# Expert numbers kept in registers, halves at the first load and the last chunk, one more engine that stores: a mixture-of-experts kernel on one core

## The chip, the core and the metric

The kernel runs on one core of a Trainium2 chip. Five engines run their own instruction streams and meet only at semaphores: TensorE (PE: matmuls and transposes; PEld is its loading of weights), VectorE (DVE), ScalarE (ACT), GpSimd (POOL) and SyncE (SP), which here issues most of the DMAs. The metric is the time of one execution in microseconds (us) on the device; lower is better. The median of three runs of the kernel before is 500.7 us (499.16 to 501.32).

## What is computed

For 4096 tokens of 256 features in 64 groups of 64 (`x`), a layer whose weight depends on the group, then a mixture of 8 experts of which each token takes 2, then a shared MLP, and the residual:

```python
# cond: h = x @ W_base.T + b_base + 2 * sum_e cond[b, e] * (x @ As[e].T) @ Bs[e].T
# As: (8, 16, 256)   Bs: (8, 256, 16)   cond_8: (64, 8)
scores = softmax(h @ gate_w.T)                      # 8 experts
topk_w, topk_i = top_k(scores, 2)
topk_w = topk_w / (topk_w.sum(-1) + 1e-20) * 2.5
g = silu(h @ w_gate[e]) * (h @ w_up[e])             # F = 352
y = sum over the 2 experts: topk_w * (g @ w_down[e])
out = x + y + (silu(h @ sw_gate) * (h @ sw_up)) @ sw_down   # 704 wide
```

## The kernel before

Every product is built from three passes over operands split in a high and a low part: `three_pass` at lines 281 to 283 (high by high, high by low, low by high). The high part is a cast by ScalarE, the low part a subtraction by VectorE. TensorE's stream has four stages.

1. Start (to about 11 us). WARM = 14 transposes of `ident` run while the first DMAs are under way (L617). Then come the transposes of `a_raw` (L622), of the first 512 tokens of x (`turn_x(0)`, L586, all of feature half k = 0 and then of k = 1), of the small inputs, the product of the base weight with the gate (L640), and the first projection. ScalarE casts each transposed half (`x_high`, L856) and then copies `gate_t`, which L640 needs. `b_raw` is turned at L650. SyncE issues x, `base_raw`, `g_raw`, `b_row`, `bias`, the second 512 tokens of x and the shared weights in this order; ScalarE's queue issues `a_raw`, `cond_in` and the two halves of `b_raw`. These two halves are read in runs of 16 floats (64 bytes).
2. The projection of the eight groups of 512 tokens (NG = 8), then the shared MLP of the first five groups (30 units: six chunks of 128 columns, the last one 64 wide, for each group), with the routing worked out beside it.
3. The expert blocks (about 182 to 412 us). The routed rows lie in NBLK = 71 blocks of 128 rows, each of one expert, whose number is in `blk_e`. One step (`e_step`) is: turn the product `g` of the block before (`e_turn_g`, L772, 3 transposes), gate and up of this block (`e_gate_up`, 12 matmuls at L281 to L283), and the down product of the block before (`e_down`, L800 and L802, 6 matmuls), which waits for `gt_l` of VectorE's L1335. Behind the gate matmuls a step also loads the next block's expert number into a register (`expert_of`), except in the last step of a turn and in the last block. Blocks 0 and 1 are written out; then a loop (`pe.Fori`) runs 5 turns of TURN = 12 steps (blocks 2 to 61), and at the head of each turn two expert numbers are loaded. Blocks 62 to 70 are written out behind two such loads.
4. The shared MLP of the last three groups (18 units), with VectorE adding up the routed rows (`sums`, L1369) beside it. The last unit is chunk 5 of group 7: `silu` (L954), the product (`mul`, L1260), the high part (`g_high`, L962), the low part (`g_low`, L1269), 8 matmuls (`down`, L722 and L723), the additions into `acc` (`final`, L1285 and twice L1281), and three stores by SyncE (L457). A chunk of 64 rows has its high part in rows 0 to 63 and its low part in rows 64 to 127 of `gt_h`, so it needs only two matmuls per 128 tokens.

The order on each engine is written out by hand; nothing is planned by a compiler.

Of the kernel before, what the change touches and what calls it, by code (L numbers as in the profile page):

```python
# [5 lines left out]
F32 = mybir.dt.float32  # L6
# [5 lines left out]
ALU = mybir.AluOpType  # L12
# [3 lines left out]
P = 128  # L16
# [5 lines left out]
def adaln_moe(nc, x, cond, w_base, b_base, lora_a, lora_b, gate_w, w_gate, w_up, w_down,  # L22
# [7 lines left out]
    K = D // P  # L30
# [9 lines left out]
    TG = GT // P  # L40
    NG = T // GT
# [13 lines left out]
    WARM = 14  # L55
# [22 lines left out]
    with ExitStack() as ctx:  # L78
# [135 lines left out]
        s_xin = [sem(f"s_xin{i}") for i in range(2)]  # L214
        s_tx, s_txh, s_txl = sem("s_tx"), sem("s_txh"), sem("s_txl")
# [28 lines left out]
        G_B, U_B, Y_B = [bank[0], bank[2]], [bank[1], bank[3]], bank[4:6]  # L244
        RANK_B, PERM_B = bank[6], bank[7]
# [57 lines left out]
        def _(sp):  # L303
# [51 lines left out]
            sp.dma_start(b_row[:], b_base.rearrange("(k p) -> k p", p=P)).then_inc(s_dc, 16)  # L355
            sp.dma_start(bias[:, 0:D], b_base.rearrange("(a o) -> a o", a=1).broadcast_to([P, D])).then_inc(s_dbias, 16)
            load_x(1)
# [221 lines left out]
        def _(pe):  # L579
# [44 lines left out]
            turn_x(0)  # L624
# [119 lines left out]

            order = [(j, c) for j in range(NG) for c in range(NC)]
# [65 lines left out]

            before = expert_of(0)
            expert = e_gate_up(0, 0, before, 1)
            down(*order[NPRE - 1])
            e_step(1, 1, before, expert, None)
            n_turns = (NBLK - 3) // TURN
            with pe.Fori(0, n_turns) as q:
                before = expert_of(q * TURN + 1)
                expert = expert_of(q * TURN + 2)
                for s in range(TURN):  # L820
                    before, expert = expert, e_step(
                        q * TURN + (2 + s), s % 2, before, expert, q * TURN + (3 + s) if s + 1 < TURN else None)
            i = n_turns * TURN + 2
            before, expert = expert_of(i - 1), expert_of(i)
# [12 lines left out]
            for last in order[-2:]:  # L837
                down(*last)

        @block.scalar  # L840
        def _(sc):
            sc.dma_start(a_raw[:], lora_a.rearrange("e r c -> (e r) c")).then_inc(s_da, 16)
            sc.dma_start(cond_in[:], cond).then_inc(s_dcond, 16)
            for k in range(K):
                sc.dma_start(b_raw[:, k, :].rearrange("p (e r) -> p e r", e=E),
                             lora_b[:, k * P:(k + 1) * P, :].rearrange("e o r -> o e r")).then_inc(s_db, 16)
# [116 lines left out]

            def r_word_high(i):
# [60 lines left out]
            for u in range(UP, UP + (NG - NPG) * NC):  # L1025
# [3 lines left out]
                if c in (1, 2) and j + 1 < NG:  # L1029
                    split(j + 1, c - 1)  # L1030

        @block.vector
        def _(v):
# [256 lines left out]

            def r_word_low(i):
# [93 lines left out]
            for n in range((NG - NPG) * NC):  # L1385
# [36 lines left out]
```

## Time and profile before

| | us |
|---|---|
| median of three runs | 500.7 |
| the profiled execution | 496.86 |
| its span, first to last instruction | 494.7 |
| TensorE matmul busy | 487.9 (99%) |
| VectorE busy | 349.6 (71%) |
| ScalarE busy | 262.2 (53%) |
| GpSimd busy | 220.3 (45%) |

The granted clock is full over the whole span. Busy time of TensorE is that of pipelined matmuls, whose ends are modelled, so it does not mean that the engine is at its peak; it does mean that gaps are few. The profiled execution took 3.8 us less than the median of the three runs.

### The profile page before, as it was taken

How to read it: one execution, taken by the hardware profiler on the slowest of the kernel's cores; microseconds unless marked ns; L12 is line 12 of the kernel's file. 1: busy time of each engine (PE TensorE's matmuls, PEld its weight loads, DVE VectorE, ACT ScalarE, POOL GpSimd, SP SyncE). 2: the span in 40 equal slices, each digit the busy share in tenths (PEclk: the TensorE clock that was granted, in tenths of full speed). 3: DMA queues.
4: the chain of work that ended last, by engine and by line, in shares of the span. 5: the costliest groups of instructions: out<-in, count | busy, mean ns of one | idle time of the engine just before them, and what ended most of it. 6: DMA issues, size and time to landing. Idle time of an engine off the chain costs nothing.

```text
span 494.7 us, 9766 instructions
## 1 busy us (share of the span) xinstructions
PE 487.9 (99%) x3071; PEld 449.3 (91%) x3072; DVE 349.6 (71%) x783; ACT 262.2 (53%) x525; POOL 220.3 (45%) x231
## 2 busy tenths in 40 slices
PE   8999999999999999999999999999999999999996
PEld 7999988888888899999999999999999999888886
DVE  3557866888887556766876776676676666379895
ACT  3577876666563445565555554555555543535322
POOL 2052238655541453565776556555555652211100
PEclk9999999999999999999999999999999999999999
DMA  8398569472222244543444444444444451699932
GB/s 230 112 294 243 172 185 316 150 219 85 44 85 44 86 98 126 121 127 107 127 119 116 116 127 117 108 127 118 111 121 123 117 112 56 176 383 302 384 139 85
DMA packets 104936, 74.53 MB, mean 151 GB/s; under 512 B 61946, under 2 KB 99844, under 8 KB 104900
## 3 DMA queue, kind: packets, MB, share of 16 engines
q1 hardware_dynamic: 95780, 55.21, 38.5%
q0 software_dynamic: 6816, 18.62, 12.8%
q10 hardware_dynamic: 2304, 0.26, 0.5%
q8 instruction: 17, 0.28, 0.3%
q14 instruction: 19, 0.16, 0.1%
HBM read 40.25 MB, written 20.32 MB: 122 GB/s over the span
## 4 chain that ended last, share of the span: by engine, by line
PE 94%; DVE 3%; issue 1%; DMA 1%; ACT 1%; DVEq 0%
PE bank L281 23%; PE bank L282 22%; PE bank L283 22%; PE bank L800 10%; PE bank L802 5%; PE bank L772 5%; PE bank L586 2%; DVE acc L1369 1%; DMA xin<-in_x_dram 1%; PE bank L598 1%; PE bank L594 1%; PE bank L595 1%; ACT gt_h L962 1%; PE bank L722 1%; DVE bank L1258 1%
## 5 line engine op out<-in xcount | busy, mean ns | idle before, releaser
L561 POOL DMA_INDIRECT y_rows<-y_sb,dst_i x71 | 69.9, 985 | 82.8 <-DVE y_sb L1344 82.8
L281 PE MATMUL bank<-w_all,rt_h 128*128 x284 | 97.5, 343 | 0.0
L283 PE MATMUL bank<-w_all,rt_l 128*128 x284 | 91.6, 323 | 0.0
L282 PE MATMUL bank<-w_all,rt_h 128*128 x284 | 91.5, 322 | 0.0
L555 POOL DMA_INDIRECT rows<-x_halves,tok_i x71 | 68.6, 967 | 25.3 <-issue 21.1
L800 PE MATMUL bank<-w_all,gt_h 128*128 (+1 forms) x213 | 78.1, 397 | 0.1
L962 ACT CAST gt_h<-bank 128x512 fp32r<-128x512 f32 (+1 forms) x48 | 28.1, 585 | 86.5 <-DVE bank L1258 77.1
L281 PE MATMUL bank<-xs_h,sg_h 128*128 128x512 f32 x176 | 70.4, 400 | 0.0
L282 PE MATMUL bank<-xs_l,sg_h 128*128 128x512 f32 x176 | 68.9, 391 | 0.0
L283 PE MATMUL bank<-xs_h,sg_l 128*128 128x512 f32 x176 | 68.7, 390 | 0.0
L1331 DVE TENSOR_TENSOR g<-bank,act 128x352 f32<-128x352 f32 x71 | 37.2, 524 | 40.2 <-ACT act L983 38.8
L978 ACT CAST gt_h<-bank 128x384 fp32r<-128x384 f32 x71 | 34.0, 479 | 59.5 <-PE bank L772 59.4
L1344 DVE TENSOR_REDUCE y_sb<-bank 128x256 f32<-128x512 f32 x71 | 49.0, 691 | 17.3 <-PE bank L802 16.2
L802 PE MATMUL bank<-w_all,gt_l 128*128 (+1 forms) x213 | 59.6, 280 | 0.0
L501 POOL TENSOR_TENSOR w_all<-w_own,w_all 128x704 fp32r<-128x704 f32 (+2 forms) x32 | 42.8, 1360 | 32.6 <-ACT w_all L874 32.6
L969 ACT COPY rt_w<-turned 128x256 uint16<-128x256 uint16 x71 | 34.6, 488 | 40.7 <-PE bank L283 29.2
L282 PEld LDWEIGHTS bank<-w_all,rt_h 128*128 128x128 f32 x284 | 53.6, 189 | 0.0
L281 PEld LDWEIGHTS bank<-w_all,rt_h 128*128 128x128 f32 x284 | 53.5, 188 | 0.1
L283 PEld LDWEIGHTS bank<-w_all,rt_l 128*128 128x128 f32 x284 | 53.4, 188 | 0.0
L1335 DVE TENSOR_TENSOR gt_l<-bank,gt_h 128x384 fp32r<-128x384 f32 x71 | 39.5, 557 | 11.5 <-ACT gt_h L978 4.6
L507 POOL TENSOR_TENSOR xs_l<-xs_w,xs_h 128x512 fp32r<-128x512 f32 x14 | 18.3, 1310 | 65.5 <-ACT xs_h L896 65.5
L800 PEld LDWEIGHTS bank<-w_all,gt_h 128*128 128x128 f32 (+1 forms) x213 | 40.0, 188 | 6.9 <-issue 0.6
(183 smaller groups left out, 1114.4 us busy)
## 6 DMA issues: line engine op xcount, KB each, us to landing
pick<-y_rows SPq DMA_DIRECT2D x16, 512.0 KB, 7.8
xin<-in_x_dram SPq DMA_DIRECT2D x8, 512.0 KB, 4.9
x_halves<-x_half SPq DMA_DIRECT2D x8, 512.0 KB, 3.3
w_own<-in_L_ffn_w_gate_dram SPq DMA_DIRECT2D x8, 352.0 KB, 4.3
w_own<-in_L_ffn_w_up_dram SPq DMA_DIRECT2D x8, 352.0 KB, 4.7
y_sb<-in_x_dram SPq DMA_DIRECT2D x5, 512.0 KB, 3.5
base_rows<-y_sb SPq DMA_DIRECT2D x5, 512.0 KB, 2.8
acc<-base_rows SPq DMA_DIRECT2D x5, 512.0 KB, 7.3
```

Of the source, the lines that this page charges most:

```text
L281: pe.matmul(o, lh, rh, start=start, stop=False, skip_group_check=skip)
L282: pe.matmul(o, lh, rl, start=False, stop=False, skip_group_check=skip)
L283: return pe.matmul(o, ll, rh, start=False, stop=stop, skip_group_check=skip)
L501: pool.tensor_tensor(lo, own_ap, hi.bitcast(F32), ALU.subtract).then_inc(s_wlo, 1)
L555: pool.indirect_dma_start(rows[i % 3][:], None, x1_dram, bass.IndirectOffsetOnAxis(ap=tok_i[:, i:i + 1], axis=0)).then_inc(s_row[i % 3], 16)
L561: pool.indirect_dma_start(y_dram, bass.IndirectOffsetOnAxis(ap=dst_i[:, i:i + 1], axis=0), y_sb[:, i % 4, :], None).then_inc(s_sc[i % 4], 16)
L800: pe.matmul(YE[par][:, 0:2 * D].rearrange("p (h d) -> p h d", h=2), gt_h[par][0:n, cols], both, start=(c == 0), stop=False, skip_group_che ...
L802: mm = pe.matmul(YE[par][:, 0:D], gt_l[par][0:n, cols], high, start=False, stop=(c == FC - 1), skip_group_check=True)
L969: sc.copy(words[:, :, :, 1], turned[i % 2][:, K:2 * K, :]).then_inc(s_rhi, 1)
L1331: v.tensor_tensor(g[:, 0:F], EU[:, 0:F], act[:, 0:F], ALU.mult).then_inc(s_g, 1)
L1335: v.tensor_tensor(gt_l[i % 2][:, 0:FC * P], TB[:, 0:FC * P], gt_h[i % 2][:, 0:FC * P].bitcast(F32), ALU.subtract).then_inc(s_gl, 1)
L1344: v.tensor_reduce(y_sb[:, i % 4, :], YE[i % 2][:, 0:2 * D].rearrange("p (h d) -> p d h", h=2), AX.X, ALU.add).then_inc(s_y, 1)
```

## The change

- TensorE keeps two expert numbers in two registers of its own. The last step of a turn now loads the next block's number too, as block 1 does, and the two numbers are moved to the kept registers at the end of a turn and read from them at the head of the next; the two loads at the head of each turn, and those behind the loop, are gone.
- x's first 512 tokens come in two DMAs of 256 tokens with a semaphore each, and are turned token tile by token tile (k inside), so that the first four transposes need the first DMA only. WARM goes from 14 to 12.
- SyncE's queue: x (two halves), `base_raw`, the second 512 tokens, `b_raw` (two), `bias`. ScalarE's: `a_raw`, `cond_in`, `g_raw`, `b_row`.
- Product, high part and low part of the last chunk are each made in two halves of 256 columns, the halves in two PSUM banks (3 and 2); the eight matmuls wait for the halves in turn.
- Of the last three stores the middle one (tile 2) is issued by ScalarE.

```diff
-    WARM = 14
+    WARM = 12
+        LAST_B = [U_B[(NC - 1) % 2], G_B[(NC - 1) % 2]]
-            load_x(0)
+            for h, got in enumerate((s_xfirst, s_xin[0])):
+                sp.dma_start(xin[0][:, h * HT:(h + 1) * HT, :],
+                             x_rows[h * HT * P:(h + 1) * HT * P, :].rearrange("(t p) d -> p t d", p=P)).then_inc(got, 16)
             sp.dma_start(base_raw[:], ...).then_inc(s_dw, 16)
-            sp.dma_start(g_raw[:], gate_w).then_inc(s_dg, 16)
-            sp.dma_start(b_row[:], ...).then_inc(s_dc, 16)
+            load_x(1)
+            for k in range(K):
+                sp.dma_start(b_raw[:, k, :]..., lora_b[:, k * P:(k + 1) * P, :]...).then_inc(s_db, 16)
             sp.dma_start(bias[:, 0:D], ...).then_inc(s_dbias, 16)
-            load_x(1)
...
-            for n, (first, end) in enumerate(((0, 2), (2, 3), (3, 4))):
+            for n, (first, end) in ((0, (0, 2)), (2, (3, 4))):
...
-            turn_x(0)
+            pe.wait_ge(s_xfirst, 16)
+            for t in range(TG):
+                if t == HT:
+                    pe.wait_ge(s_xin[0], 16)
+                for k in range(K):
+                    mm = pe.transpose(TX[k][:, t * P:(t + 1) * P], xin[0][:, t, k * P:(k + 1) * P], ident[:])
+                    if t == TG - 1:
+                        mm.then_inc(s_tx, 1)
...
+            def down_last():
+                j, c = NG - 1, NC - 1
+                u, p = unit(j, c), c % 2
+                for h in range(2):
+                    pe.wait_ge(s_gl, u + 1 + h)
+                    for t in range(2 * h, 2 * h + 2):
+                        ...
+                    mm.then_inc((s_first, s_D)[h], 1)
...
+            def keep(*es):
+                for r, e in zip(kept, es):
+                    pe.reg_mov(r, pe.to_reg(e))
+            def as_kept():
+                return [pe.snap(r, min_val=0, max_val=E - 1) for r in kept]
-            e_step(1, 1, before, expert, None)
+            keep(expert, e_step(1, 1, before, expert, 2))
             with pe.Fori(0, n_turns) as q:
-                before = expert_of(q * TURN + 1)
-                expert = expert_of(q * TURN + 2)
+                before, expert = as_kept()
                 for s in range(TURN):
-                    ... q * TURN + (3 + s) if s + 1 < TURN else None)
+                    ... q * TURN + (3 + s))
+                keep(before, expert)
-            before, expert = expert_of(i - 1), expert_of(i)
+            before, expert = as_kept()
...
+            def g_high_last(h):
+                sc.wait_ge(s_g, u + 1 + h)
+                sc.wait_ge(s_D, u - 1)
+                sc.copy(gt_h[p][0:HALF, cols], LAST_B[h][0:HALF, cols]).then_inc(s_gh, 1)
+            sc.wait_ge(s_fin, 2 * (NG - 1) + 2)
+            sc.dma_start(out_rows[r:r + P, :]..., acc[NG - 1][:, 2:3, :]).then_inc(s_out, 16)
...
+            def mul_last(h):
+                v.wait_ge(s_act, u + 1)
+                v.tensor_tensor(LAST_B[h][0:HALF, cols], G_B[p][HALF:P, cols], act[HALF:P, cols], ALU.mult).then_inc(s_g, 1)
+            def g_low_last(h):
+                v.wait_ge(s_gh, u + 1 + h)
+                v.tensor_tensor(gt_h[p][HALF:P, cols], LAST_B[h][0:HALF, cols], gt_h[p][0:HALF, cols].bitcast(F32),
+                                ALU.subtract).then_inc(s_gl, 1)
```

## Rows read from the trace of the kernel before

**Rows 1.** The page, chain of work that ended last, by engine.

```profile
PE 94%; DVE 3%; issue 1%; DMA 1%; ACT 1%; DVEq 0%
```

**Rows 2.** TensorE's waits: who waited for whom, us in total, times, longest.

```profile
PE bank L772 <- issue: 1.2, 4, 0.5
```

**Rows 3.** Timeline of the start: start, us, engine, line, operation, [idle before <-releaser].

```profile
1.47 3.25 PE L617 MATMUL bank<-ident 128*128 128x128 f32 x14 [1.47 <-POOL ident L472]
1.85 1.23 ACTq L845 DMA_DIRECT2D b_raw<-in_L_cond_Bs_dram  x2
5.34 1.87 PE L586 MATMUL bank<-ident,xin 128*128 128x128 f32 x8 [0.19 <-DMA xin<-in_x_dram]
7.25 0.58 ACT L856 CAST xt_h<-bank 128x512 fp32r<-128x512 f32 x1 [0.17 <-PE bank L586]
...
8.11 0.96 PE L640 MATMUL bank<-gate_t,base_raw 128*128 128x8 f32 x8
...
11.84 0.38 PE L650 MATMUL bank<-ident,b_raw 128*128 128x128 f32 x2
```

**Rows 4.** DMA views: b's two halves (KB, us to landing); SyncE's queue from 0 to 4.

```profile
b_raw<-in_L_cond_Bs_dram ACTq DMA_DIRECT2D x1, 64.0 KB, 4.8
...
b_raw<-in_L_cond_Bs_dram ACTq DMA_DIRECT2D x1, 64.0 KB, 8.4
...
q1 hardware_dynamic: 299, 0.31, 22.0%
```

**Rows 5.** Windows of two steps, TensorE: stretch and its length, busy (x), clock, DMA, GB/s.

```profile
184.91:192.34 7.43, 6.90 (x44) 1.00 0.57 160
...
225.43:232.55 7.12, 6.82 (x44) 1.00 0.49 128
265.58:272.48 6.90, 6.83 (x45) 1.00 0.49 131
305.51:312.54 7.03, 6.86 (x44) 1.00 0.43 116
345.64:352.64 7.00, 6.84 (x44) 1.00 0.48 122
385.75:392.37 6.62, 6.62 (x44) 1.00 0.43 117
```

**Rows 6.** Timeline, the low part and the next transposes, at three places.

```profile
226.30 0.56 DVE L1335 TENSOR_TENSOR gt_l<-bank,gt_h 128x384 fp32r<-128x384 f32 x1
...
229.02 0.54 PE L772 MATMUL bank<-ident,g 128*128 128x128 f32 x3 [0.30 <-issue]
...
386.62 0.56 DVE L1335 TENSOR_TENSOR gt_l<-bank,gt_h 128x384 fp32r<-128x384 f32 x1
...
388.88 0.49 PE L772 MATMUL bank<-ident,g 128*128 128x128 f32 x3
...
407.22 0.56 DVE L1335 TENSOR_TENSOR gt_l<-bank,gt_h 128x384 fp32r<-128x384 f32 x1
...
409.08 0.49 PE L772 MATMUL bank<-ident,g 128*128 128x128 f32 x3
```

**Rows 7.** Queues of instruction fetches: the whole span (page), then 230 to 388 us.

```profile
q8 instruction: 17, 0.28, 0.3%
...
q14 instruction: 8, 0.07, 0.1%
```

**Rows 8.** Timeline of the end.

```profile
489.26 0.68 DVE L1269 TENSOR_TENSOR gt_h<-bank,gt_h 64x512 fp32r<-64x512 f32 x1 [0.65 <-ACT gt_h L962]
...
489.99 0.39 PE L722 MATMUL bank<-sd_h,gt_h 128*128 128x256 f32 x1 [0.31 <-DVE gt_h L1269]
...
491.45 0.75 DVE L1281 TENSOR_TENSOR acc<-bank,acc 128x256 f32<-128x256 f32 x2
491.56 1.39 SPq L457 DMA_DIRECT2D out_dram<-acc  x3
```

**Rows 9.** Windows at the end: busy of five engines (x), clock, DMA share, GB/s.

```profile
493.00:493.50 0.50, 0.00 (x0) 0.00 (x0) 0.00 (x0) 0.00 (x0) 0.00 (x0) 1.00 1.11 385
```

More of the change, by code:

```diff
@@ L40, in adaln_moe @@
     TG = GT // P
+    HC = GT // 2
+    HT = TG // 2
     NG = T // GT
@@ L810, in e_step @@
                 return e_next
+            kept = [pe.alloc_register(f"expert{n}") for n in range(2)]
+            def keep(*es):
[3 more added lines that the diff above has]
+                return [pe.snap(r, min_val=0, max_val=E - 1) for r in kept]
             before = expert_of(0)
@@ L814, in _ @@
             down(*order[NPRE - 1])
-            e_step(1, 1, before, expert, None)
+            keep(expert, e_step(1, 1, before, expert, 2))
             n_turns = (NBLK - 3) // TURN
             with pe.Fori(0, n_turns) as q:
-                before = expert_of(q * TURN + 1)
-                expert = expert_of(q * TURN + 2)
+                before, expert = as_kept()
                 for s in range(TURN):
-                    before, expert = expert, e_step(
-                        q * TURN + (2 + s), s % 2, before, expert, q * TURN + (3 + s) if s + 1 < TURN else None)
+                    before, expert = expert, e_step(q * TURN + (2 + s), s % 2, before, expert, q * TURN + (3 + s))
+                keep(before, expert)
             i = n_turns * TURN + 2
-            before, expert = expert_of(i - 1), expert_of(i)
+            before, expert = as_kept()
             for n in range(i, NBLK):
@@ L836, in _ @@
                 up(j, c)
-            for last in order[-2:]:
-                down(*last)
+            down(*order[-2])
+            down_last()
         @block.scalar
@@ L843, in _ @@
             sc.dma_start(cond_in[:], cond).then_inc(s_dcond, 16)
-            for k in range(K):
-                sc.dma_start(b_raw[:, k, :].rearrange("p (e r) -> p e r", e=E),
-                             lora_b[:, k * P:(k + 1) * P, :].rearrange("e o r -> o e r")).then_inc(s_db, 16)
+            sc.dma_start(g_raw[:], gate_w).then_inc(s_dg, 16)
+            sc.dma_start(b_row[:], b_base.rearrange("(k p) -> k p", p=P)).then_inc(s_dc, 16)
             sc.wait_ge(s_ident, 1)
@@ L1024, in _ @@
             e_high(NBLK - 1)
-            for u in range(UP, UP + (NG - NPG) * NC):
+            for u in range(UP, UP + (NG - NPG) * NC - 1):
                 j, c = NPG + (u - UP) // NC, (u - UP) % NC
@@ L1030, in _ @@
                     split(j + 1, c - 1)
+            silu(NG - 1, NC - 1)
+            for h in range(2):
+                g_high_last(h)
+            sc.wait_ge(s_fin, 2 * (NG - 1) + 2)
+            r = (NG - 1) * GT + 2 * P
+            sc.dma_start(out_rows[r:r + P, :].rearrange("(t p) d -> p t d", p=P), acc[NG - 1][:, 2:3, :]).then_inc(s_out, 16)
         @block.vector
@@ L1384, in _ @@
                        (7, 2): [(7, 5, 8), (4, 0, 3)], (7, 3): [(4, 4, 8)]}
-            for n in range((NG - NPG) * NC):
+            for n in range((NG - NPG) * NC - 1):
                 j, c = NPG + n // NC, n % NC
@@ L1396, in _ @@
                     sums(*some_of)
+            for h in range(2):
+                mul_last(h)
+            for h in range(2):
+                g_low_last(h)
             v.wait_ge(s_mix, TOPK * TG * (NG - NPG))
```

11 lines of the change are left out of this document (10 added, 1 removed).

## The prediction

> **What bounds the kernel now.** I read the page's chain of work that ended last first: 94% of it is TensorE [rows 1]. So what the change can give is what TensorE's stream loses somewhere, plus the ends, where TensorE has not yet begun or is already done. TensorE's list of waits names few losses in the middle: 1.2 us of "issue" in 4 places before L772, that is, waits for nothing that another engine or a DMA does [rows 2]. The timelines of both ends and windows of equal work around the loop's turns give the sizes.
>
> **The loop's turns.** A window over two steps (from one step's transposes to those of the step after next) shows what a turn's head costs. Behind the loop, where two expert numbers are loaded as well but nothing jumps back, two steps take 6.62 us. The four jumps back take 7.12, 6.90, 7.03 and 7.00, together 28.05 against 26.48: 1.57 us over. The entry to the loop takes 7.43, 0.81 over [rows 5]. Together 2.38 us. Half of it is the gap, half the slower start behind it: three transposes take 0.54 behind a gap and 0.49 (of which the next matmuls cover more) elsewhere [rows 6].
>
> Is it the loads? From the end of the low part, on which `e_down` waits, to the next transposes it is 229.02 - 226.86 = 2.16 us at a turn; 388.88 - 387.18 = 1.70 behind the loop, with two loads and no gap; and 409.08 - 407.78 = 1.30 in a step whose `e_down` came late, with neither loads nor jump [rows 6]. I read this so: the instruction stream goes on from the wait in `e_down`, and needs at most 1.30 us for six matmuls and the way to the transposes; two loads, the loop's compare and jump, and the arithmetic on the loop's register add 0.86 or more. TensorE itself arrives after 1.70, so about 0.46 must go for the gap to vanish. The change takes away two loads with their address arithmetic and adds four register moves. Bounds: if the loads carry nothing, the gain is 0 (or below: a few moves more, 0.1 each at most for four jumps and the entry, -0.5); if they carry 0.46 or more, all 2.38 goes. The row behind the loop says that loop control alone is at least 2.16 - 1.70 = 0.46, so the loads' share lies between 0 and 2.16 - 0.46 less the matmuls' own issue. Twelve to fifteen instructions in that 1.30 can hardly fill it, since TensorE takes 0.12 for each there anyway; I take 0.3 per load and its arithmetic, 0.6 for two, and 0.1 back for the moves: the stream is then ready at 1.66, just ahead of TensorE. I enter 2.2 of 2.38. The twelfth step's new load lies behind the gate matmuls as those of the other eleven, which show no loss.
>
> A rule of the Trainium skill speaks against this. "Runtime: NRT & Kernel Launch", section Instruction fetch mechanics, says that code is prefetched in sequence and that a taken jump to code outside the window stalls until the page is fetched; the stall would then be the jump's and stay. In this trace the only queue of instruction fetches from 230 to 388 us is q14 with 8 packets, while q8, with 17 packets of 16 KB over the span, has none there; so no fetch by TensorE goes with the jumps, if q8 is its queue [rows 7]. "Advanced Engine Details and Errata", section Control Flow Timing, has about 108 ns for compare-and-branch, and the Runtime page about 200 ns for one register load (from HBM, not SBUF); an estimate by these two is 0.4 less per turn and 2.16 - 0.4 + moves = 1.8, still a small gap and the slower start, and the loop would give about 0.9.
>
> **The start.** TensorE turns x from 5.34, when the whole DMA has landed, in 8 slots of 0.23 (1.87), and ScalarE's second cast ends at 7.83; behind it come `gate_t` and L640 at 8.11, and from there TensorE runs without a gap [rows 3]. After: twelve transposes instead of fourteen (3.25 for 14) and `a_raw`'s two end near 4.55. The first 256 tokens are 256 packets of 1 KB, and SyncE's queue had moved 299 by 4.0 us [rows 4]; the whole of x (512) landed near 5.3. I put the first half's landing at 4.5, between 4.0 and 5.3. Four slots run to 5.5, the second half is there, four more end near 6.6. Feature half k = 0 is now whole only one slot before k = 1, so ScalarE's two casts run one behind the other, 6.4 to 7.45, against 7.83: 0.38 us gained, not the 0.6 by which the transposes end earlier. If the first half lands with the second, the eight slots stay where they are and k = 0 comes later: the second cast ends near 8.1, 0.27 lost. If the faster pace seen from L640 on (0.96 for 8) comes later than before because less ran ahead of it, up to 0.2 goes as well.
>
> `b_raw` moves from ScalarE's queue (issues from 1.85) behind 1.28 MB on SyncE's, issued from about 2.7. Its landing took 4.8 and 8.4 us [rows 4], the second while it shared the DMA engines with SyncE's bulk. It is needed at 11.84 - 0.38 = 11.46 [rows 3]. With 8.4 from 3.3 it lands at 11.7, 0.25 late; with 4.8 at 8.1. In the new order it stands alone between the second x and `bias`, so I take nothing, and keep -0.25. `g_raw` and `b_row` stand behind 130 KB on ScalarE's queue and are needed near 6.6; `base_raw` is issued 0.45 later and needed near 7: nothing. SyncE's shared weights are needed only after 20 us. Whatever is gained here is carried on, since TensorE bounds all that follows.
>
> **The end.** TensorE has a gap of 0.31 before L722, waiting for L1269, and its first slot is 0.23 instead of 0.12; with the slot that ran out before it the last eight matmuls could begin at 489.42 + 0.12 = 489.53 instead of 489.99, and the loss is 0.46 + 0.11 = 0.57 [rows 8]. Halves: VectorE 0.33 to 0.42 for 256 columns (two L1281 in 0.75) instead of 0.68 for 512 (L1269) [rows 8]; for ScalarE I take 0.42 too. Three whole steps of 512 columns end at 489.94, so they began near 487.9. From there the product's first half ends at 488.32, the high part's near 488.8, the low part's near 489.25 and the second low part's near 489.6, needed at 490.0. So TensorE has no gap: 0.57 gained. The stores: SyncE issues three in 1.39, 0.46 each, from 491.56; the third goes at 492.49, though its rows were ready at 492.2 [rows 8]. With ScalarE issuing the middle one, the third issue goes at 491.63 + 0.03: 0.83 earlier. But the 512 KB take 1.36 us at 385 GB/s [rows 9] from the first store on, and that one moves by 0.57 only. I take 0.57 for the end, 0.83 as its upper bound. (The Trainium skill, "DMA: Bandwidth & Descriptors", section Issuing engines are not separate DMA queues, says that a second issuing engine saves issue time only; that row agrees so far.) If the halves cost a bank wait or a slow semaphore, 0.3 is left.
>
> **Sum.** 2.2 + 0.38 + 0.57 = 3.15 us off the profiled 496.86, that is 493.7. The profiled execution lies 3.84 under the median of 500.7, and I take the same difference off the median: 497.5 (-0.6%). A measurement of this kernel can tell about 0.5%, 2.5 us, from no change, so the forecast is just beyond it.
>
> **Rivals.**
> 1. The jump and not the loads makes the gaps (or the moves cost what the loads did). For it: the two loads behind the loop cost nothing seen. Against it: the entry, which jumps back from nowhere, loses most. Then the loop gives 0.5 and the sum is 1.45: 499.3. Chance 0.23.
> 2. The first half lands with the second: the start loses 0.27 instead, sum 2.5: 498.2. For it: both halves run over the same 16 engines, and all of x took until 5.3 though 299 of 512 packets were through at 4.0. Against: those 299 already include a whole half. Chance 0.15.
> 3. Slower: `b_raw` on SyncE's queue. TensorE's stream stops at L650 until it lands, and with it `lora_out` and all that follows. At 11.46 it begins to cost; from 14.6, 11.3 us after its issue, it eats all 3.15 us. The 8.4 seen says no, but a queue that stands still for 2048 packets of 64 B would also hold the shared weights behind it. With the landing at 16: 502.1. Chance 0.04.
> 4. The change does nothing that can be seen, because the gains in TensorE's stream are given back by a wait for rows or weights from DRAM that don't come earlier. TensorE's list of waits shows no such wait now [rows 2]. 500.5, chance 0.06.
> The forecast keeps 0.52. Its own range, from the bounds above and the spread of the runs, is 496.3 to 498.8; with the rivals I give 495.8 to 500.2. Faster by over 0.5% (under 498.2): most of the forecast, half of rival 2 and a little of rival 1, 0.54. Within 0.5%: 0.42. Slower: 0.04.
>
> **What would show it.** Windows over two steps across each jump should read 6.62 to 6.7 and the entry no more than 6.7; if they stay at 7.0, rival 1. The transposes of x should begin before 4.8 and L640 near 7.75; a wait for x's first half until 5.3 is rival 2. L650 should follow its neighbour without a gap; else rival 3. The last chunk's L722 should have no gap, the third store's issue should begin near 491.66 less what came earlier, and the data should end 0.57 earlier relative to TensorE's last unit. The prediction is wrong if the two-step windows away from the jumps grow, since they are 99% of the time.

## The result and the profile after

The changed kernel takes 493.74 us (median of 6 runs, 492.86 to 499.03); the kernel before, beside it on the same chip, 499.93 (497.01 to 501.32). The ratio is 0.9895, 95% interval 0.9855 to 0.9935. The forecast was 497.5, and 493.74 lies 2.1 us under the low end of its range. Ratios and differences of means, here and below, leave out executions more than 1.5% above the fastest of the same kernel; medians are of all. The six spans of the changed kernel are 495.0, 491.5, 491.0, 492.3, 497.2 and 491.4: four close together and two that are 3.5 and 6 us longer. The profiled execution is one of the two long ones (496.81, span 495.0), so its span of 495.0 beside the 494.7 of before says nothing until it is taken apart.

The start, from the timeline (start, us, engine, line, operation, [idle before <-releaser]); it answers to [rows 3]:

```profile
4.57 3.03 SPq L366 DMA_DIRECT2D bias<-in_L_cond_b_base_dram  x1
...
4.70 1.65 PE L640 MATMUL bank<-ident,xin 128*128 128x128 f32 x8
...
6.27 1.07 ACT L895 CAST xt_h<-bank 128x512 fp32r<-128x512 f32 x2 [0.96 <-PE bank L640]
...
11.33 0.38 PE L668 MATMUL bank<-ident,b_raw 128*128 128x128 f32 x2
```

x is turned from 4.70 instead of 5.34, both casts run one behind the other until 7.34 (forecast 7.45), and the transposes of `b_raw` stand at 11.33 without a gap, 0.51 earlier than in [rows 3]. TensorE's first expert step begins at 184.25; it was 184.74.

The loop, from windows of TensorE alone (stretch and length, busy (x), granted clock, DMA share, GB/s); they answer to [rows 5]. Each is two steps, except those of 5.07 and 5.08, which are one:

```profile
184.25:191.12 6.87, 6.87 (x44) 1.00 0.55 155
191.12:197.91 6.79, 6.79 (x45) 1.00 0.34 97
197.91:202.98 5.07, 3.47 (x23) 1.00 0.63 137
...
222.85:229.47 6.62, 6.62 (x44) 1.00 0.44 119
262.57:269.19 6.62, 6.62 (x44) 1.00 0.45 120
299.03:304.11 5.08, 3.46 (x23) 1.00 0.49 142
304.11:310.76 6.65, 6.65 (x43) 1.00 0.28 86
343.79:350.40 6.61, 6.61 (x45) 1.00 0.43 119
```

The turns' heads read 6.62, 6.62, 6.65 and 6.61 where they read 7.12, 6.90, 7.03 and 7.00 (these windows begin one step earlier than those of [rows 5]; the step behind each head is 3.30 too): the heads cost nothing now. The entry reads 6.87 instead of 7.43. But the next two steps take 6.79, and then one step alone takes 5.07 instead of 3.30; a second such step comes at 299. TensorE's list of waits has both:

```profile
PE bank L803 <- DVE g L1394: 3.2, 2, 1.6
```

The last two batches below turn on these long steps. Here is the one at 198 (timeline of ScalarE, VectorE and TensorE):

```profile
198.16 0.41 PE L286 MATMUL bank<-w_all,rt_h 128*128 x1
...
200.76 0.46 ACT L1028 ACTIVATE act<-bank 128x352 f32<-128x352 f32 x1 [1.44 <-PE bank L288]
...
202.40 0.53 DVE L1394 TENSOR_TENSOR g<-bank,act 128x352 f32<-128x352 f32 x1 [2.46 <-issue]
...
202.98 0.55 PE L803 MATMUL bank<-ident,g 128*128 128x128 f32 x3 [1.60 <-DVE g L1394]
```

In step 2 the first gate matmul begins at 187.89 and `act` at 189.14, 1.25 later; here `act` begins 2.60 later. So what is late is the signal of TensorE's own gate product, 1.35 us, and then the up product's; VectorE and TensorE's next transposes only pass it on. TensorE's matmul records of this step stand 0.16 apart as always, and their ends are modelled: the records don't show where in the step TensorE stood.

The end, from the timeline; it answers to [rows 8]:

```profile
489.58 0.76 DVE L1351 TENSOR_TENSOR gt_h<-bank,gt_h 64x256 fp32r<-64x256 f32 x2
...
490.21 0.28 PE L288 MATMUL bank<-sd_h,gt_l 128*128 128x256 f32 x1
490.33 0.28 PE L772 MATMUL bank<-sd_h,gt_h 128*128 128x256 f32 x1
...
491.69 0.74 DVE L1333 TENSOR_TENSOR acc<-bank,acc 128x256 f32<-128x256 f32 x2
491.80 1.01 SPq L467 DMA_DIRECT2D out_dram<-acc  x2
492.14 0.38 ACTq L1082 DMA_DIRECT2D out_dram<-acc  x1
```

The last eight matmuls follow the unit before without a gap. From its last matmul to the span's end it is 4.79 (495.0 - 490.21), where it was 494.7 - 489.41 = 5.29: 0.50 gained.

Taken apart: 0.51 (start), 1.55 (four heads, 28.05 - 26.50), 0.38 at the entry and the steps behind it (0.70 less in step 1, from 4.09 to 3.39, and 0.32 more in steps 2 to 4, from 9.95 to 10.27), 0.50 (end), and 0.34 for one step at 405 us that took 3.64 before and 3.30 now: 3.28, so 494.7 - 3.28 = 491.4. That is the span of the four short executions (491.0 to 492.3), which I read as those without a long step; only the long one was profiled. It has two, 3.55 us: 495.0.

### The profile page after: what moved, and what is told of

Same layout as the page of the kernel before. It is cut to its first block, busy times and chain, and to the rows that moved or that the text cites. A ratio compares the mean times of both kernels' runs of the same rounds, so it can differ in the third digit from the quotient of the medians.

```text
span 495.0 us, 9758 instructions
## 1 busy us (share of the span) xinstructions
PE 486.6 (98%) x3069; PEld 448.7 (91%) x3070; DVE 349.8 (71%) x785; ACT 261.8 (53%) x526; POOL 220.3 (45%) x231
## 4 chain that ended last, share of the span: by engine, by line
PE 93%; DMA 2%; DVE 2%; issue 1%; ACT 1%; SPq 0%; POOL 0%; DVEq 0%; another core or an unknown queue 0%; POOLq 0%
PE bank L286 22%; PE bank L288 22%; PE bank L287 22%; PE bank L831 10%; PE bank L833 5%; PE bank L803 5%; DMA pick<-y_rows 1%; PE bank L596 1%; PE bank L608 1%; PE bank L604 1%; DMA y_rows<-y_sb,dst_i 1%; PE bank L605 1%; PE bank L741 1%; PE bank L740 1%; DVE acc L1432 1%
## 5 line engine op out<-in xcount | busy, mean ns | idle before, releaser
L1407 DVE TENSOR_REDUCE y_sb<-bank 128x256 f32<-128x512 f32 x71 | 49.0, 690 | 17.4 <-issue 9.7
```

The source lines that it names most:

```text
L1407: v.tensor_reduce(y_sb[:, i % 4, :], YE[i % 2][:, 0:2 * D].rearrange("p (h d) -> p d h", h=2), AX.X, ALU.add).then_inc(s_y, 1)
```

## The experiments

"Step" is the distance between the transposes of two blocks, 3.30 us where nothing disturbs; "step 5" is the fifth of them, at about 198 us. Each batch has its own runs of the kernel before; a single run is given with its span.

### First batch: the same two kernels, the loop alone, and the price of a load

again_before is the kernel before, again_after the changed one, unaltered.

> The kernel before once more, timed against itself. Theory A (each execution of either kernel carries a random number of stalls of about 1.6 us each in the expert blocks, as at 202 and 304 us in the changed kernel's profile, and the profiled execution of before had none): times from 496.8 to 502 in steps of about 1.6 us, ratio within 0.4% of 1, and the profile shows TensorE waiting for g (L1331) at other places than any other execution, or not at all. Theory B (the kernel before stalls in most executions, because of its instruction stream): a median near 500 again and a profile with 2 or more such waits. Both say that the lowest time is near 496.8.

505.04 us median (499.98 to 513.42; 12 runs), and 503.17 for the 29 runs of the same kernel beside it: this chip has longer and more scattered times. The profiled execution (508.92) is one of its longer ones, and has five long steps:

```profile
PE bank L772 <- DVE g L1331: 7.5, 5, 1.9
PE bank L772 <- issue: 1.6, 4, 0.6
```

Three of the four waits in the second row are the entry and two heads again, as in [rows 2]; the longest, 0.62, stands in a step of 4.08 at 217 us. The first row doesn't exist in the profile of before that the forecast was made from.

The start differs too, and by more than anything that the change was meant to do. TensorE waits longer for x, and then goes on at half the pace (first again_before, then the profile of before):

```profile
5.79 1.97 PE L586 MATMUL bank<-ident,xin 128*128 128x128 f32 x8 [0.64 <-DMA xin<-in_x_dram]
...
11.44 0.63 PE L595 MATMUL bank<-xt_h,at_l 128*128 128x512 f32 x1
11.87 0.63 PE L594 MATMUL bank<-xt_h,at_h 128*128 128x512 f32 x1
```

```profile
9.24 0.39 PE L595 MATMUL bank<-xt_h,at_l 128*128 128x512 f32 x1
9.47 0.39 PE L594 MATMUL bank<-xt_h,at_h 128*128 128x512 f32 x1
```

Its matmuls of 512 columns stand 0.43 apart where those of before stand 0.23 apart, until about 13.6 us; the clock column reads 1.00 in both. The transposes of `b_raw` come at 15.06 instead of 11.84, the first expert step at 187.99 instead of 184.74: 3.25 us.

> The changed kernel once more. By the windows of its profile the three parts give 0.5 (start), 2.1 (loop) and 0.5 (end), and a stall of 0.3 near 407 us is gone: 3.4 us. Theory A: the lowest time 492.9 to 493.4, the mean of many runs 3.4 to 4 us under that of before, ratio 0.992 to 0.993. Theory B (the change also takes away stalls): mean and median 5 to 6 us lower, ratio 0.988 to 0.990, and the upper half of its times stays below 495.

498.99 (495.53 to 508.06; 12 runs), ratio 0.9946 (0.9904 to 0.9989). Three long steps (TensorE waits 4.7 us for `g` in them), one of them step 5 again, and two shorter ones, 3.97 and 4.00. So both kernels have long steps, of 0.7 to 2.1 us each, and the profiled execution of before happened to have none. The start of this execution is a fast one: `b_raw` at 11.08, the first expert step at 184.02, 3.97 before again_before's.

loop_only is the kernel before with the change to TensorE's loop alone:

```diff
+            keep(expert, e_step(1, 1, before, expert, 2))
             with pe.Fori(0, n_turns) as q:
-                before = expert_of(q * TURN + 1)
-                expert = expert_of(q * TURN + 2)
+                before, expert = as_kept()
...
+                keep(before, expert)
```

> Only the experts kept in registers; start, last chunk and stores as before. Theory (the loads at the head are the gaps): windows over two steps across each jump read 6.62 instead of 6.90 to 7.12 and the entry about 6.9 instead of 7.43; 2.1 us less. Rival (the jump itself makes the gap): 7.0 at the jumps, under 0.6 us less. If stalls became rarer by this part alone, the median would drop by 5.

501.12 (495.7 to 504.13; 10 runs), ratio 0.997 (0.9922 to 1.0018). No head loses anything, but step 5 takes 4.94, and two more 4.72 and 4.22. This kernel has the start of before, and its profile shows the half pace again: a wait of 0.64 for x, and the first expert step at 188.40.

loads_four loads two more expert numbers at each head of the kernel before, and uses all four, so that none can be dropped:

```diff
+                before2 = expert_of(q * TURN + 1)
+                expert2 = expert_of(q * TURN + 2)
                 before = expert_of(q * TURN + 1)
                 expert = expert_of(q * TURN + 2)
+                again.update(up=expert2, down=before2)
```

> Before, with two more loads of an expert number at the head of each turn (four in all), whose values are used. If a load at the head costs 0.3 us as I took it, the windows across the jumps go from 7.0 to 7.6; if a load costs next to nothing (0.05), to 7.1. The entry goes from 7.43 to 8.0 or 7.5.

508.54 (span 506.4). The heads' steps are 4.42, 4.37, 4.52 and 4.58; with two loads they are 3.76, 3.53, 3.64 and 3.63. That is 3.33 us for eight loads, **0.42 us for each load** with its arithmetic. The one at 231 as a window:

```profile
231.22:235.64 4.42, 3.47 (x23) 1.00 0.38 101
```

So the gap grows with the loads, and is gone without them (rival 1 falls). The loop has a share all the same: behind the loop the same two loads, with no jump, leave the two steps at 6.62 [rows 5]. This execution, with the start of before, is the third with the half pace (a wait of 0.64 for x, first expert step at 188.15). The slack that TensorE has there follows too: two loads cost 0.84 of stream time and about 0.34 of TensorE's time, so some 0.5 is hidden, near the 0.46 of [rows 6]. The Trainium skill, "Runtime: NRT & Kernel Launch", section Instruction fetch mechanics, gives about 200 ns for a register load from HBM; these, from SBUF with the address worked out beside them, cost twice that.

### Second batch: the parts by themselves

start_only has the change's two edits of the start, x_only the split x (with WARM 12) on the old queues, b_only the new queues with x in one piece, halves_only the last chunk in halves with all stores by SyncE. All else is as before.

```diff
 start_only = x_only + b_only
 x_only:      x in two DMAs of 256 tokens, turned tile by tile; WARM = 12
 b_only:      b_raw and the second x on SyncE's queue, g_raw and b_row on ScalarE's
 halves_only: mul_last, g_high_last, g_low_last, down_last
```

> Only the start: x in two loads with its transposes token tile by token tile, WARM 12, and the moved DMAs. Predicted 0.38 us, seen in the whole change about 0.51 at L650 (11.84 to 11.33). Expected here the same 0.51 at the transposes of b_raw, and nothing else: turns of the loop 6.9 to 7.1, gap before L722 of 0.31.

> Only x in halves with WARM 12; all queues as before. If the gain of the start is that of the halves, the transposes of b_raw begin near 11.3 as in the whole change, unless b_raw is late: its second half landed at 10.87 before. If moving b_raw mattered (its small packets share the DMA engines with x), the first transposes of x begin later than 4.70 and the gain is under 0.4.

> Only the queues: b_raw on SyncE's queue behind the second x, g_raw and b_row on ScalarE's. x lands whole as before, so its transposes begin at 5.3 and L640 near 8.1: gain 0. b_raw lands at 8 to 9 instead of 10.9. SyncE is held for some 3 us at bias, which costs nothing since the next thing that it brings is needed after 13 us.

> Only the last chunk in halves, three stores by SyncE. TensorE has no gap before its last eight matmuls (0.31 before); from the end of the last full product (L283 at 489.41 before) to the end of the span it was 5.29 us. Theory (data on the DMA engines bounds the stores): 4.8, as in the whole change. Rival (SyncE's issues bound them): 4.8 only with ScalarE's store, about 5.0 here.

The single times are 496.16, 496.04, 496.14 and 494.73 (spans 494.0, 493.9, 494.0, 492.9) beside 496.48 for before; they are too close to be told apart as times, and the timelines tell more. The transposes of `b_raw` stand at 10.93 in start_only, 11.32 in x_only and 11.87 in b_only, against 11.84 before. Against before the queues alone gain nothing, the split x 0.5. Why both together gain 0.4 more than x_only shows in its trace:

```profile
6.57 0.29 PE L644 MATMUL bank<-ident,g_raw 8*128 8x8 f32 x2 [0.75 <-DMA g_raw<-in_L_ffn_gate_w_dram]
```

TensorE comes to `g_raw` earlier than the old queue delivers it. The step "nothing" that the forecast entered for `g_raw` is right only because the same change moves it. But single executions of one start differ by as much. In four profiles with x in one piece (before, b_only, halves_only, end_only) the `b_raw` transposes stand between 11.47 and 11.87, 11.67 in the mean; in eleven with both edits between 10.47 and 11.33, 11.00 in the mean. In these eleven the transposes of x begin between 4.45 and 4.70 each time; what differs is their pace, 1.04 us (0.12 each) to 1.91 (0.23 each) for the eight. A third group is the three of the first batch with x in one piece: `b_raw` at 15.1 to 15.4. So the new start is worth 0.67 on the average beside the first four, and 4 us beside an execution in which TensorE keeps the half pace. That was seen in three of seven profiles with x in one piece, all on one chip, and in none of thirteen with x in halves, of which one is from that chip. All three have a wait of 0.64 for x, the other four none or one of at most 0.27; that the wait causes it is likely by this, and not tested. But for one step of 4.24 at 404 us in start_only, these four profiles have no long steps, as that of before.

For the end, the distance from SyncE's first store issue to the span's end tells what the store by ScalarE is worth: 3.14 before (491.56 to 494.7), 3.18 in halves_only (489.72 to 492.9), 3.20 in the changed kernel (491.80 to 495.0). **Nothing.** The view of DMAs from 493 to 495 in the changed kernel (busy tenths and GB/s in 40 slices; queues with packets, MB and share) says why: the engines move 350 to 430 GB/s until the last packet, from both queues together.

```profile
DMA  9999999999999999999996400000000000000000
GB/s 389 389 430 348 410 389 348 430 369 348 410 348 369 430 369 369 389 348 389 389 430 205 144 21 0 0 0 0 0 0 0 0 0 0 0 0 0 0 0 0
...
q1 hardware_dynamic: 317, 0.29, 41.9%
q10 hardware_dynamic: 144, 0.13, 18.9%
```

The three issues end 0.38 earlier (1.01 instead of 1.39), and the bytes wait behind each other. The halves give the whole gain: from the last full product to the end it is 4.77 in halves_only and 4.79 in the changed kernel, 5.29 before. The Trainium skill, "DMA: Bandwidth & Descriptors", section Issuing engines are not separate DMA queues, agrees: a second issuer saves issue time, not bandwidth.

### Third batch: the changed kernel on another chip, one load, shorter turns, the end alone

after_third is the changed kernel unaltered. load_one adds `expert = expert_of(q * TURN + 2)` at each head of the changed kernel. turn_six has TURN = 6, so ten heads and not five. end_only is the kernel before with the halves and ScalarE's store.

> The changed kernel on another chip, in five rounds beside the kernel before. On the second chip the means lay 3.1 us apart (503.7 and 500.6) with stalls in both, on the first 4.6. Theory A (equally many stalls in both): means 3.4 us apart within 1.5, and lowest times 3.4 to 4 apart. Theory B (fewer in the changed kernel): means 5 or more apart. The three profiles with kept experts all have a stall in step 5 (near 202 us); if that belongs to the kernel and not to chance, it is here too.

498.21 (495.31 to 504.7; 12 runs), ratio 0.9924 (0.9882 to 0.9965); step 5 takes 4.89.

> The changed kernel with one expert number loaded at the head of each turn again, in place of the kept one. Four loads at the head gave steps of 4.47 us on average where two gave 3.64, so 0.42 a load. The stream is then ready 0.42 earlier than with two loads (2.05 after the low part), at 1.63 or with the moves 1.7, just when TensorE is: steps at the heads 3.30 to 3.45. Rival (the loop's compare and jump wait for the pipeline whatever is loaded): 3.5 or more.

509.85 (span 508.0), with 3.36, 3.39 and 3.37 at three heads and one of its long steps, 5.04, at the fourth. That fits one load (0.42) within TensorE's slack, as the 0.5 above asks, but weakly: each of the three heads stands right behind a step of 3.94 or 3.95. At the entry, which nothing precedes, one load shows: step 1 is 3.64, with none 3.39, with two 4.09, with four 4.95. Steps 2 to 5 are 3.43, 4.01, 3.38 and 3.30. This execution has so many long steps (17.9 us over 3.30 in its 70 steps) that its time says nothing of the load; why it has so many stays open.

> The changed kernel with TURN = 6: ten jumps back instead of four (blocks 2 to 67 in eleven turns). If a jump without loads costs nothing, no step at a head is over 3.35 and the expert blocks take as long as with TURN = 12; if it costs 0.1 each, they take 0.6 longer.

503.14 (span 501.3). Ten heads and none of them loses (3.30 to 3.43): the price of a head without loads is 0 for either number of turns. The Trainium skill's rule that I had set against the change ("Runtime: NRT & Kernel Launch", section Instruction fetch mechanics: a taken jump to code outside the window stalls until the code is fetched) has no stall to explain here; whether the loop's code lies outside that window no run shows. Its five long steps gave a sight of the clock. Right behind the one at 289.2, windows of TensorE read:

```profile
293.00:295.00 2.00, 0.31 (x4) 1.00 0.57 129
296.00:299.00 3.00, 3.00 (x12) 0.50 0.38 108
...
388.50:391.00 2.50, 2.50 (x10) 0.50 0.30 82
392.50:394.00 1.50, 1.50 (x12) 1.00 0.10 38
```

TensorE waits 2.06 us for a product, and soon after its granted clock is 0.50 (the 1.2 GHz level) for some 3 us, with matmuls 0.29 apart; the step takes 4.92. The second place (388.5) follows waits of 0.31 and 1.47 in one step, and load_one has a third at 410 us, behind a wait of 1.75, with a step of 4.90. The long steps that stand alone are as long (4.9 to 5.1), but show 1.00 in that row, and behind a wait of 1.95 in again_before it reads 1.00 as well. Whether they too are run at the lower level with the record missing it, I can't say.

> Only the end: last chunk in halves and ScalarE's store; loop and start as before. Against halves_only, whose stores all come from SyncE, this shows what ScalarE's store brings: 0.2 to 0.3 if SyncE's issues set the end, under 0.1 if the 512 KB on the DMA engines do. The loop's heads stay at 3.5 to 3.8.

501.43 (span 499.6), with two long steps (5.18, 5.09), two shorter ones (4.25, 4.10), and a first store issue 3.2 before the end. Before has 501.92 there.

### Fourth batch: is step 5 the change's?

Up to here step 5 was long in all five profiles of kernels with kept numbers whose heads have no load, and in none of the eight with two or more loads at the heads (again_before has a long step 6); load_one, with one, has a step 3 of 4.01. Four kernels were run on one chip: after_fourth, the changed kernel; no_loop, the changed kernel with the loop of before; entry_gap, which puts two loads back ahead of the loop alone; and x_order.

```diff
-            keep(expert, e_step(1, 1, before, expert, 2))
+            e_step(1, 1, before, expert, None)
+            keep(expert_of(1), expert_of(2))
```

> The changed kernel once more, beside the three below. All theories: 3.0 to 4.7 us under the kernel before, as on the other chips. Theory C (TensorE driven without the gap at the loop's entry runs into one long step right behind it): a step of 4.8 to 5.2 us among the first six, as in three profiles of this kernel so far. Rival (long steps fall at random): that place is a coincidence, and this profile has none there with a chance of about one half.

496.82 (495.0 to 500.89; 12 runs) against 498.27 (29 runs), ratio 0.9957 (0.9926 to 0.9989). Step 5 takes 4.10: late again, but less than the 4.8 to 5.2 that theory C asks.

> The changed kernel with the loop of before (two loads at each head and behind the loop). Theory A (the parts add up, long steps are independent of the change): 0.51 us of the start and 0.50 of the end are left, so 1.0 under before and 2.0 to 2.4 over the changed kernel; the heads' steps 3.55 to 3.75 and the entry's about 4.1. Theory C (the kept numbers give 2.2 back at the gaps but cost a long step of 1.6 to 1.8 behind the entry): only 0.4 to 0.6 over the changed kernel, and no long step among the first six.

496.94 (494.14 to 498.26; 13 runs), ratio 0.9961 (0.9932 to 0.999). Its mean is 0.21 under the changed kernel's, with a 95% interval of -1.23 to +0.64: theory A's +2.0 to +2.4 is out, and C's +0.4 to +0.6 is in. On this chip **the kept numbers gave back all that they gained at the heads.** The heads read as in [rows 5], and steps 3 to 6 read 3.30:

```profile
183.42:190.85 7.43, 6.91 (x45) 1.00 0.58 160
190.85:197.45 6.60, 6.60 (x44) 1.00 0.36 101
```

> The changed kernel with the two loads put back ahead of the loop alone, so that TensorE has its 0.8 us at the entry again and nowhere else. Theory A (independent): the entry's step is 4.0 to 4.1, the four turns' heads stay at 3.3, the time is 0.8 over the changed kernel. Theory C (the missing gap brings the long step): no long step among the first six, and the time is 0.8 to 1.0 under the changed kernel.

494.76 (493.48 to 497.77; 12 runs), ratio 0.9922 (0.989 to 0.9954); its mean is 1.96 under the changed kernel's (95%: -3.13 to -0.87). The only step over 3.36 is the entry's, 4.33. So a gap of 0.8 us put back made the kernel 2 us faster. Against no_loop, which has the same gap and pays at the heads too, its mean is 1.75 lower (95%: 0.8 to 2.6): about the 1.55 of the heads, which are a gain once the entry is left as it was.

> The changed kernel with the second half of x's transposes again feature half by feature half (both tiles of k = 0, then both of k = 1), so that ScalarE can cast k = 0 two slots earlier. If the cast of k = 1 sets the start: the last transpose is where it was, the first cast begins 0.25 to 0.45 us earlier but the second only by what it waited behind the first, 0.1 to 0.3, and the transposes of b_raw come as much earlier (11.33 in the changed kernel). If the transposes of x set it: nothing, within 0.05.

This one has the second half's transposes again feature half by feature half. 498.6 (span 496.8, ten steps over 3.42; here step 6 is the long one, 5.10). TensorE waits 0.35 for `g_raw`, and the `b_raw` transposes stand at 11.52, not earlier; ScalarE's casts begin at 6.03 and end at 7.10, 0.24 before those of the first profile. The cast is not what set 11.33, or `g_raw` hides it; no more than that can be read from it.

### Fifth batch: a gap or only a delay?

entry_fill puts eight transposes of `ident` where entry_gap has its loads, so that TensorE is late but never idle. entry_gap_again is entry_gap once more; its chip turned out to be the same one, at another time.

```diff
             keep(expert, e_step(1, 1, before, expert, 2))
+            for _ in range(8):
+                pe.transpose(bank[3][:, 0:P], ident[:], ident[:])
```

> The changed kernel with eight more transposes of ident (0.12 us each, 0.96 in all, into a PSUM bank that nothing uses then) between block 1 and the loop: TensorE is as late at the loop's first step as with the two loads of entry_gap, but it doesn't stand still. Order theory (without the 0.8 us TensorE's e_down runs into VectorE's low part, which stands behind a reduction that waits for a DMA, and the two stay out of step until the long step 5): steps 2 to 4 at 3.30 instead of 3.40 to 3.54, no long step among the first six, and the time as entry_gap's within 0.5, that is 3.0 to 4.0 under before. Idle theory (the long step 5 comes where TensorE has worked too long without a pause): steps 2 to 4 may be 3.30, but a step of 4.8 to 5.2 among the first six stays, and the time is 1.2 to 2.0 over entry_gap.

493.21 (492.89 to 493.74; 5 runs) against 496.35 (495.67 to 497.05; 9 runs), ratio 0.9943 (0.9929 to 0.9956). The idle theory falls: TensorE is delayed here without standing still, and there is no long step; what the order theory expected is there, but for its time against entry_gap_again (below). Windows of TensorE in entry_fill:

```profile
183.96:191.55 7.59, 7.59 (x53) 1.00 0.76 158
191.55:198.15 6.60, 6.60 (x44) 1.00 0.36 101
198.15:204.76 6.61, 6.61 (x44) 1.00 0.46 119
221.28:227.88 6.60, 6.60 (x44) 1.00 0.49 119
```

> The kernel with the two loads ahead of the loop alone, on another chip. If its 1.96 us under the changed kernel there were its own: 3.2 to 4.2 us under before (3.7 in the mean there), steps 2 to 4 at 3.30 and no long step among the first six. If they were an accident of the chip or of the place of long steps: 2.0 to 3.0 under before, and a long step as likely among the first six as in any other six of the 70.

494.14 (493.5 to 494.86; 5 runs), ratio 0.9959 (0.9945 to 0.9973), no long step in its profile, mean 2.14 under before (less than the 3.2 forecast), and 0.86 over entry_fill (95%: 0.37 to 1.36), where the order theory had them within 0.5. Of the 1.0 between the two profiled spans 0.38 lies ahead of the first expert step and 0.54 among the steps; why is open. Here all nine runs of before lie within 495.67 to 497.05, so this gain is one with few long steps on either side. Each of the two beats the kernel before; that entry_gap beats the changed kernel is measured side by side in the fourth batch, that entry_fill does is not.

What the order is, VectorE's timeline shows. First the changed kernel's reductions (L1407), which stand ahead of the low parts on VectorE:

```profile
188.64 0.69 DVE L1407 TENSOR_REDUCE y_sb<-bank 128x256 f32<-128x512 f32 x1 [1.07 <-DMA base_rows<-y_sb]
...
191.33 0.69 DVE L1407 TENSOR_REDUCE y_sb<-bank 128x256 f32<-128x512 f32 x1 [0.43 <-PE bank L833]
...
195.37 0.69 DVE L1407 TENSOR_REDUCE y_sb<-bank 128x256 f32<-128x512 f32 x1 [0.69 <-PE bank L833]
...
198.11 0.69 DVE L1407 TENSOR_REDUCE y_sb<-bank 128x256 f32<-128x512 f32 x1 [0.29 <-PE bank L833]
```

Then entry_fill's:

```profile
188.33 0.69 DVE L1409 TENSOR_REDUCE y_sb<-bank 128x256 f32<-128x512 f32 x1 [1.00 <-DMA base_rows<-y_sb]
...
191.74 0.69 DVE L1409 TENSOR_REDUCE y_sb<-bank 128x256 f32<-128x512 f32 x1
...
195.05 0.69 DVE L1409 TENSOR_REDUCE y_sb<-bank 128x256 f32<-128x512 f32 x1 [0.25 <-PE bank L833]
```

In both the first reduction waits 1.0 us for a DMA. In entry_fill the delay of TensorE takes that in, and the reductions come 3.3 apart from then on. In the changed kernel they come 2.7, 4.0 and 2.7 apart. Part of that is TensorE's own doing: in step 3 VectorE makes `g` 2.81 us behind the transposes, waiting for the up product, where it is 2.51 in a quiet step (that at 232.77). So the product's signal is late by 0.30 there already, as it is by 1.35 and more in step 5. `e_down`, which needs the low part behind the reduction, hardly moves (2.31 behind the transposes in step 2, 2.26 in step 3, 2.25 in a quiet step).

Over all twenty profiles, the seven of kernels whose entry has neither loads nor delay have a long step (4.10 to 5.13) among steps 2 to 6, and of the thirteen others two have one: again_before (5.15) and load_one (4.01). That a delay of TensorE at the entry prevents it is shown, and that it need not be idle time. That it works through the order between TensorE and VectorE is read from the spacing above and not tested by itself, and how a product's signal comes to be late is open.

## Why the prediction was right and wrong

**The sum was near, its base was wrong.** The forecast took 3.15 off the profiled 496.86 and had 493.7 there; the median is 493.74. What failed is the step after it: "I take the same difference off the median: 497.5". The changed kernel doesn't carry that difference: its median lies 3.8 us under the forecast, at the time of an undisturbed execution, and its profiled execution is 3.07 above its median where that of before is 3.84 below. Four of its first six executions were short. An offset that comes from events of single executions isn't a constant of the kernel, and the range should have reached down to the sum itself, 493.7.

What the 3.84 of before was made of stays open, since only the short execution was profiled. Two kinds of events on record have the size: two long steps of 1.8 us, which both kernels have, or one start at half pace (3.25 to 3.66 us in three profiles), seen with the start of before alone. By the first the median fell by luck of the draw; by the second the change took the cost away, and the term of the start, 0.38, was far too small. The forecast saw that a faster pace sets in at L640 and priced its coming later at no more than 0.2.

That 493.7 and 493.74 agree to 0.04 is luck in any case. The 3.28 found in the profile has 0.34 of an accident in it, which stands in for the 0.27 that the loop fell short, and the medians of the two kernels differ by 6.2, not by 3.15.

**What the change is worth in the mean** is near the forecast all the same. The means over the four comparisons with before differ by 4.65, 3.15, 4.01 and 1.74 us, on average 3.4 (95%: 2.5 to 4.2), where 3.15 was forecast. That the first was the highest of the four is no more than chance as far as these runs can tell.

**The loop: 2.2 forecast.** At the heads 1.57 was there, and 1.55 gained, more surely than argued, since a load costs 0.42 and not 0.3. At the entry the rest was forecast, of 0.81 seen there. Step 1 gained 0.70; steps 2 to 4 gave back 0.32, and step 5, wherever it was long, 0.8 to 1.8. The forecast did not ask what would be late once the entry's gap was gone. Its own sign of being wrong, windows away from the jumps that grow, came true in steps 2 to 5 (6.79 and 5.07). In the first comparison the loop brought 1.9 in the profile but for its long steps, in the fourth batch nothing.

**The start: 0.38 forecast, 0.51 came** in the first pair of profiles, 0.67 between the means of undisturbed ones, and about 4 us against an execution at half pace. The first half was there by 4.70 at the latest, well ahead of 5.3, so rival 2 falls. `b_raw` cost nothing: its two DMAs took 5.2 us in the median, and rival 3 falls. What stands behind them on SyncE's queue came later: the issue of `bias` held it for 3.03 us, and the shared weights were issued at 7.65 instead of 3.85. Nobody needed them before 20 us.

**The end: 0.57 forecast, 0.50 came**, all through the halves; that ScalarE's store brings nothing was the forecast's bound of 385 GB/s [rows 9].

**Not foreseen:** 0.34 us of one step at 405, an accident of the profiled execution as it seems: at that place start_only has 4.24 and no_loop 3.30.

Rival 4, gains given back by a wait, had 0.06 and named rows or weights from DRAM. Gains were given back at another place, behind the loop's entry, and on one chip that took half of the gain; what was late there was TensorE's own products, not rows or weights.

## What to carry over

Before the difference between a profile and the median is added to a forecast, ask what it is made of: look in the trace for single events, and if the profiled execution has none of them, forecast the undisturbed time too and let the range reach it. Profile more than one execution of the kernel before: the next one, again_before, has a start at half pace that costs more than any term of the sum. Where a stall is taken out ahead of a loop, look at who used it to catch up: here 0.8 us of delay at TensorE kept the next steps quiet, and without it TensorE lost more than that within five steps. A load of a register at a loop's head costs what it takes beyond the engine's own lead, here 0.42 each beyond 0.5; the jump without loads cost nothing.

## What the runs showed of the hardware

- Both kernels have single steps that are 0.6 to 2.2 us too long, without a wait for another engine's work: the signal of TensorE's own product is late while its records keep their spacing. Chips and times differ from none (all nine runs of before within 495.67 to 497.05) to five waits in one execution (7.5 us). What they are stays open.
- Behind three such steps, with waits of 2.06 and 1.47 us (turn_six) and 1.75 (load_one), the granted clock was 0.50 for some 3 us though TensorE was busy, at 1.6 us for the step; behind a wait of 1.95 (again_before) it stayed at 1.00.
- In three executions in which TensorE waited 0.64 us for x at 5.2 to 5.8 us it went on at half its later pace (512 columns in 0.43 instead of 0.23) until about 13.6 us, and its first expert step came 3.25 to 3.66 us later than in the profile of before; with waits of at most 0.27 the full pace was there from L640 on, at 8.1 (before). The clock column reads 1.00 in both.
- The issue behind the two DMAs of `b_raw` on SyncE's queue took 2.3 to 3.7 us instead of 0.36. The second 512 tokens of x stand ahead of it as well there, so that the short runs (2048 of 64 bytes) are the reason is not shown.
